# The transposed one-hots of a graph kernel: PE transposes and ACT copies, or DVE comparisons with keys from a DMA

## What is computed

```python
x_i = x[dst]                                   # (25000, 48)
x_j = x[src]
tmp = jnp.concatenate([x_i, x_j, edge_attr], axis=1)      # 48 + 48 + 32 = 128
h = jax.nn.relu(tmp @ W1 + b1)                 # (25000, 128)
msg = h @ W2 + b2                              # (25000, 48)
out = jax.ops.segment_sum(msg, dst, num_segments=100000)
y = _layernorm(x + out, axis=-1)               # eps = 1e-5
```

## Time and profile before

| | |
|---|---|
| median of 3 runs | 494.03 us |
| span of the profiled execution | 593.7 us |
| PE, PE weight loads | 430.8 us, 368.5 us busy |
| DVE, POOL, ACT | 383.0, 351.2, 292.1 us busy |
| granted TensorE clock, mean | 0.937 |
| first loads of edges, last ones | 30.2 us, 551.6 us |

### The profile page before, as it was taken

One profiled execution on the slowest core, in us unless ns is written; L12 is line 12 of the kernel. 1 busy time (PEld: TensorE's weight loads), 2 busy tenths in 40 slices (PEclk: granted clock), 3 DMA queues, 4 the chain that ended last, 5 costly groups with the idle time before them and its releaser, 6 DMA issues.

```text
span 593.7 us, 19546 instructions
## 1 busy us (share of the span) xinstructions
PE 430.8 (73%) x6796; PEld 368.5 (62%) x6796; DVE 383.0 (65%) x1105; ACT 292.1 (49%) x795; POOL 351.2 (59%) x365
## 2 busy tenths in 40 slices
PE   1013378797888878788788878787888878887891
PEld 1012367676767767676667767675776767766690
DVE  5423148676766678676667666776667756877673
ACT  2212147464555556464555545464555545554662
POOL 2056616767665666666665666666666666757522
PEclk9999999988988899898989888989889989999996
DMA  7833313444433434344444344343443434444422
GB/s 181 286 64 67 68 25 82 86 110 87 110 84 81 108 84 108 83 108 82 100 89 94 94 83 108 81 109 82 88 100 83 108 83 107 86 108 85 105 64 73
DMA packets 118243, 56.92 MB, mean 96 GB/s; under 512 B 46019, under 2 KB 117185, under 8 KB 118205
## 3 DMA queue, kind: packets, MB, share of 16 engines
q1 hardware_dynamic: 109440, 48.35, 32.2%
q0 software_dynamic: 8448, 6.50, 8.6%
q10 hardware_dynamic: 318, 1.61, 1.0%
HBM read 33.80 MB, written 22.61 MB: 95 GB/s over the span
## 4 chain that ended last, share of the span: by engine, by line
PE 66%; issue 18%; another core or an unknown queue 6%; ACT 4%; DVE 3%; DMA 1%; ACTq 0%; POOL 0%; SPq 0%; POOLq 0%; DVEq 0%
PE bank L839 14%; PE bank L827 11%; PE bank L819 10%; PE bank L779 8%; PE bank L805 8%; PE bank L858 7%; PE bank L773 7%; ACT onehot_t L899 2%; DMA next_dst_i<-in_dst_dram 1%; PE bank L851 1%; ACT sq L926 1%; ACT hid_t L915 1%; ACT cat L921 0%; ACT msg L894 0%
## 5 line engine op out<-in xcount | busy, mean ns | idle before, releaser
L732 POOL DMA_INDIRECT cat<-in_x_dram,cat x264 | 267.9, 1015 | 201.1 <-DMA cat<-edge_table 135.7
L899 ACT ACTIVATE onehot_t<-bank 128x384 bf16<-128x384 bf16 (+1 forms) x261 | 119.3, 498 | 182.1 <-remote 129.4
L1024 DVE TENSOR_REDUCE total<-bank 128x9 f32<-128x432 f32 (+1 forms) x88 | 52.8, 599 | 87.6 <-remote 86.5
L839 PE MATMUL bank<-x_low,onehot_t 128*128 128x48 bf16 (+1 forms) x782 | 86.0, 185 | 27.4 <-issue 26.9
L839 PE MATMUL bank<-x_rest,onehot_t 128*128 128x48 bf16 (+1 forms) x782 | 85.8, 186 | 26.7 <-issue 26.6
L858 PEld LDWEIGHTS bank<-w,hid_t 128*128 128x128 f32 x522 | 101.5, 208 | 4.0 <-issue 2.8
L779 PEld LDWEIGHTS bank<-ident_b,onehot 128*128 128x128 bf16 (+1 forms) x782 | 65.2, 107 | 61.4 <-issue 48.1
L839 PE MATMUL bank<-xs,onehot_t 128*128 128x48 bf16 (+1 forms) x782 | 86.6, 186 | 22.5 <-issue 22.1
L779 PE MATMUL bank<-ident_b,onehot 128*128 128x128 bf16 (+1 forms) x782 | 80.6, 236 | 24.9 <-issue 24.9
L740 POOL TENSOR_TENSOR ys<-ys,rstd 128x432 f32<-128x432 f32 (+1 forms) x88 | 80.3, 912 | 23.6 <-DVE rstd L1090 20.5
L858 PE MATMUL bank<-w,hid_t 128*128 128x48 f32 x522 | 89.9, 255 | 2.5 <-issue 2.5
(11 more groups left out here) (91 smaller groups left out, 910.8 us busy)
## 6 DMA issues: line engine op xcount, KB each, us to landing
xs<-in_x_dram SPq DMA_DIRECT2D x86, 216.0 KB
out_dram<-ys SPq DMA_DIRECT2D x86, 216.0 KB
cat<-edge_table SPq DMA_DIRECT2D x264, 17.0 KB
cat<-in_x_dram,cat POOLq DMA_INDIRECT x264
edge_table<-table_pm SPq DMA_DIRECT2D x4, 833.0 KB, 7.5
edge_pm<-in_edge_attr_dram ACTq DMA_DIRECT2D x2, 686.0 KB, 6.0
edge_pm<-in_edge_attr_dram SPq DMA_DIRECT2D x2, 686.0 KB, 6.0
edge_pm<-in_edge_attr_dram ACTq DMA_DIRECT2D x2, 91.9 KB, 7.3
```

The costliest lines, as they stand in the source:

```text
L732: pool.indirect_dma_start(cat[:, v, k, D:2 * D], None, x[:, :], bass.IndirectOffsetOnAxis(ap=cat[:, v, k, P + 1:P + 2].bitcast(I32), axis= ...
L839: last = pe.matmul(xdst_ps[:, k * D:(k + 1) * D], onehot_t[0:n, v % SMALL, k, j * P:(j + 1) * P], part[:, (k * jj + j) * D:(k * jj + j + 1 ...
L899: act.activation(onehot_t[0:n, v % SMALL, k, 0:jj * P], onehot_ps[k % 2][0:n, 0:jj * P], ACT.Copy).then_inc(onehot_t_ready, 1)
L1024: dve.tensor_reduce(total[0:n, v % SMALL, 0:blocks * jj], sums_of(g, v % SMALL), AX_X, ALU.add).then_inc(totalled, 1)
```

## The change

The transposed one-hot no longer comes from the one-hot. onehot_t[node, edge] is 1 where the edge's destination is the node, and DVE makes it by a comparison: it needs the edges' destinations along the free dimension, the same in all partitions. So the set-up part writes the destinations, each modulo 768 (two blocks, CYCLE), as float16 to a DRAM row key_line. For each block SP then loads 128 keys from key_line, spread over the 128 partitions, into keys: three more DMAs for a super, issued in turn with those of edge_table. DVE compares them with the node that a partition stands for (node_col, short_col), for two supers at once (PAIR): six comparisons of 128x384 in every second step, make_onehot_t. It stands in DVE's list where place_dst stood, second.

Since the keys are modulo two blocks, place_dst goes: edge_table holds the key in place of the destination, and make_onehot compares it with the even or the odd half of node_of. turn_onehots, turn_last_onehot, copy_onehots and copy_last_onehot leave the lists of PE and ACT, and the two PSUM banks fall free. fetch_xdst reads onehot_t in its new layout. The flag for the general path is also set if two neighbouring blocks have fewer than 128 edges together, because a key could then match a node two blocks on. The set-up part gets nine more DVE instructions ahead of the table's last column, three more ahead of the flag, one more for constants, and one DMA (key_line).

```diff
+KEY_SLOTS = 4
...
+    PAIR = 2
+    CYCLE = 2 * BLOCK
...
+    key_line = nc.dram_tensor("key_line", (ROWS,), F16, kind="Internal").ap()
...
+        keys = sb("keys", [P, KEY_SLOTS, PAIR * SUPER, P], F16)
...
-        dst_in_block = sb("dst_in_block", [P, SMALL, SUPER])
...
-        onehot_t = sb("onehot_t", [P, SMALL, SUPER, J * P], BF16)
+        onehot_t = sb("onehot_t", [P, SMALL, J, PAIR * SUPER, P], BF16)
...
             sp.wait_ge(cols_placed, 2)
+            sp.dma_start(key_line.rearrange("(p t) -> p t", p=P), key_rows_h[:, :]).then_inc(table_out, 16)
...
-            sp.wait_ge(table_out, 16 * TCH)
+            sp.wait_ge(table_out, 16 * TCH + 16)
...
+                half, pair = v % PAIR, v // PAIR
+                s, q = pair % KEY_SLOTS, pair // KEY_SLOTS + r * (BODY // PAIR // KEY_SLOTS)
                 firsts = numbers(first_edge[0:1, bass.ds(super_row(g) * 4, SUPER)])
                 for k in range(SUPER):
 
                     first = firsts[first_place(g) + min(k, blocks - 1)]
                     sp.dma_start(cat[:, v, k, 2 * D:P + META], edge_table[bass.ds(first, P), :]).then_inc(row_in[v], 16)
+                    sp.dma_start(keys[:, s, half * SUPER + k, :],
+                                 key_line[bass.ds(first, P)].rearrange("(a e) -> a e", a=1).broadcast_to([P, P])).then_inc(keys_in[s], 16)
...
+                pe.wait_ge(onehot_ready, g + 1)
...
-            def turn_block(g, v, k):
-                n, blocks, jj = shape_of(g)
-                for j in range(jj):
-                    last = pe.transpose(onehot_ps[k % 2][0:n, j * P:(j + 1) * P], onehot[:, v, k, j * n:(j + 1) * n],
-                                        ident_b[:, :])
-                last.then_inc(onehot_turned, 1)
-
-            def turn_onehots(g, r, v):
-
-                n, blocks, jj = shape_of(g)
-                pe.wait_ge(onehot_ready, g + 1)
-                if after(g, 1):
-                    pe.wait_ge(onehot_t_ready, first_block(g))
-                for k in range(min(blocks, 2)):
-                    turn_block(g, v, k)
-
-            def turn_last_onehot(g, r, v):
-
-                n, blocks, jj = shape_of(g)
-                if blocks == SUPER:
-                    pe.wait_ge(onehot_t_ready, first_block(g) + 1)
-                    turn_block(g, v, 2)
...
-                pe.wait_ge(onehot_t_ready, first_block(g) + blocks)
+                pair, half = v // PAIR, v % PAIR
+                pe.wait_ge(onehot_t_ready, g - half + PAIR)
                 for k in range(blocks):
                     for j in range(jj):
                         for i, part in enumerate(parts):
-                            last = pe.matmul(xdst_ps[:, k * D:(k + 1) * D], onehot_t[0:n, v % SMALL, k, j * P:(j + 1) * P],
+                            last = pe.matmul(xdst_ps[:, k * D:(k + 1) * D], onehot_t[0:n, pair % SMALL, j, half * SUPER + k, :],
...
-            walk(pe, ((2, turn_cat), (0, turn_onehots), (5, sums), (2, hidden), (0, turn_last_onehot), (1, fetch_xdst),
-                      (3, messages)))
+            walk(pe, ((2, turn_cat), (5, sums), (2, hidden), (1, fetch_xdst), (3, messages)))
...
-            def copy_block(g, v, k):
-                n, blocks, jj = shape_of(g)
-                act.wait_ge(onehot_turned, first_block(g) + k + 1)
-                act.activation(onehot_t[0:n, v % SMALL, k, 0:jj * P], onehot_ps[k % 2][0:n, 0:jj * P],
-                               ACT.Copy).then_inc(onehot_t_ready, 1)
...
-            walk(act, ((7, root), (2, copy_cat), (4, copy_msg), (0, copy_onehots), (6, square), (0, copy_last_onehot), (2, relu),
-                       (1, place_xdst)))
+            walk(act, ((7, root), (2, copy_cat), (4, copy_msg), (6, square), (2, relu), (1, place_xdst)))
...
-            dve.tensor_copy(table_pm[:, :, DE], dst_rows[:, 0:EC]).then_inc(cols_placed, 1)
+            note(dve.tensor_scalar(key_rows[:, :], dst_rows[:, 0:EC], N - 0.5, None, ALU.min))
+            note(dve.tensor_scalar(cycle_i[:, :], key_rows[:, :], 1.0 / CYCLE, None, ALU.mult))
+            note(dve.tensor_copy(cycle_f[:, :], cycle_i[:, :]))
+            note(dve.scalar_tensor_tensor(out=key_rows[:, :], in0=cycle_f[:, :], scalar=-float(CYCLE), in1=key_rows[:, :],
+                                          op0=ALU.mult, op1=ALU.add))
+            note(dve.tensor_scalar(cycle_f[:, :], key_rows[:, :], 0.0, float(CYCLE), ALU.is_lt, ALU.mult))
+            note(dve.tensor_tensor(key_rows[:, :], key_rows[:, :], cycle_f[:, :], ALU.add))
+            note(dve.tensor_scalar(cycle_f[:, :], key_rows[:, :], float(CYCLE), -float(CYCLE), ALU.is_ge, ALU.mult))
+            note(dve.tensor_tensor(key_rows[:, :], key_rows[:, :], cycle_f[:, :], ALU.add))
+            note(dve.tensor_copy(key_rows_h[:, :], key_rows[:, :]))
+            dve.tensor_copy(table_pm[:, :, DE], key_rows[:, :]).then_inc(cols_placed, 1)
...
+            note(dve.tensor_tensor(pair_counts[:, 0:NB - 2], first_row[:, 2:NB], first_row[:, 0:NB - 2], ALU.subtract))
+            note(dve.tensor_reduce(sparse[:, :], pair_counts[:, 0:NB - 2], AX_X, ALU.min))
+            note(dve.scalar_tensor_tensor(out=crowded[:, :], in0=sparse[:, :], scalar=P - 0.5, in1=crowded[:, :],
+                                          op0=ALU.is_lt, op1=ALU.add))
...
-            def place_dst(g, r, v):
-
+            def make_onehot(g, r, v):
                 n, blocks, jj = shape_of(g)
                 dve.wait_ge(row_in[v], 16 * SUPER * (r + 1))
-                dve.tensor_tensor(dst_in_block[:, v % SMALL, 0:blocks], cat[:, v, 0:blocks, P],
-                                  block_start[:, bass.ds(first_block(g), blocks)], ALU.subtract).then_inc(dst_counted, 1)
-
-            def make_onehot(g, r, v):
-                n, blocks, jj = shape_of(g)
-                nodes = node_of if jj == J else short_node_of
-                dve.wait_ge(dst_counted, g + 1)
                 if after(g, BODY):
                     dve.wait_ge(sum_done, g - BODY + 1)
                 for k in range(blocks):
-                    last = dve.tensor_scalar(onehot[:, v, k, 0:n * jj], nodes[:, 0:n * jj],
-                                             dst_in_block[:, v % SMALL, k:k + 1], None, ALU.is_equal)
+                    odd = (v * SUPER + k) % 2
+                    nodes = node_of[:, odd * BLOCK:(odd + 1) * BLOCK] if jj == J else short_node_of[:, :]
+                    last = dve.tensor_scalar(onehot[:, v, k, 0:n * jj], nodes, cat[:, v, k, P:P + 1], None, ALU.is_equal)
                 last.then_inc(onehot_ready, 1)
...
+            def make_onehot_t(g, r, v):
+
+                if v % PAIR:
+                    return
+                pair = v // PAIR
+                s, q = pair % KEY_SLOTS, pair // KEY_SLOTS
+                dve.wait_ge(keys_in[s], 16 * PAIR * SUPER * (r * (BODY // PAIR // KEY_SLOTS) + q + 1))
+                t = pair % SMALL
+                if after(g, PAIR * SMALL):
+                    dve.wait_ge(xdst_done, g - PAIR * (SMALL - 1))
+                blocks = sum(shape_of(g + i)[1] for i in range(PAIR)) if isinstance(g, int) and g >= NS - PAIR else PAIR * SUPER
+                full = blocks if blocks == PAIR * SUPER else blocks - 1
+                for odd in range(2):
+                    for j in range(J):
+                        last = dve.tensor_scalar(onehot_t[:, t, j, odd:full:2, :], keys[:, s, odd:full:2, :],
+                                                 node_col[:, odd * J + j:odd * J + j + 1], None, ALU.is_equal)
+                if full < blocks:
+                    for j in range(RJ):
+                        last = dve.tensor_scalar(onehot_t[0:RP, t, j, SUPER, :], keys[0:RP, s, SUPER, :],
+                                                 short_col[0:RP, j:j + 1], None, ALU.is_equal)
+                last.then_inc(onehot_t_ready, PAIR)
...
-            walk(dve, ((6, total_sum), (-1, place_dst), (-1, less_high_x), (6, centre), (-1, less_middle_x),
+            walk(dve, ((6, total_sum), (-1, make_onehot_t), (-1, less_high_x), (6, centre), (-1, less_middle_x),
```

More of the change, by code:

```diff
@@ L418, in gnn_resnorm_kernel @@
     FAR = 1 << 20
+    PAIR = 2
+    CYCLE = 2 * BLOCK
+    assert PAIR * KEY_SLOTS == BODY and (PAIR * SUPER) % 2 == 0 and BODY % PAIR == 0 and NS % PAIR == 0 and CYCLE <= 2048
     BG = 100
@@ L476, in gnn_resnorm_kernel @@
         ident_b = sb("ident_b", [P, P], BF16)
-        node_of_i = sb("node_of_i", [P, BLOCK], I32)
-        node_of = sb("node_of", [P, BLOCK], F16)
+        node_of_i = sb("node_of_i", [P, CYCLE], I32)
+        node_of = sb("node_of", [P, CYCLE], F16)
         short_node_of = sb("short_node_of", [P, REST], F16)
-        block_start = sb("block_start", [P, NB])
-        block_start_i = sb("block_start_i", [P, NB], I32)
+        node_col_i = sb("node_col_i", [P, 2 * J], I32)
+        node_col = sb("node_col", [P, 2 * J])
+        short_col_i = sb("short_col_i", [P, RJ], I32)
+        short_col = sb("short_col", [P, RJ])
+        key_rows = sb("key_rows", [P, EC])
```

(27 more changed lines are left out.)

9 lines of the change are left out of this document (4 added, 5 removed).

## The result

The changed kernel takes 628.4 us (median of 4 runs, 627.07 to 630.51) where the kernel before takes 494.25 us beside it: a ratio of 1.2742, 95% interval [1.2697, 1.2786]. The forecast was 586 us, with a range of 510 to 630. Sign and mechanism are as predicted; the size is 42 us beyond the forecast's centre, at the upper end of its range.

The account below looks back on a forecast made before the run. It took POOL (4.99 us a step) as the bound, SP 0.3 us behind; with SP's new step of 6.1 us, start 31 + 87 steps 531 - 7 without stores + tail 31 gave 586 us, range 510 to 630.

Parts of the forecast that it names:

- (c): SP gains three DMA issues a step, 1.44 us, taking its step from 4.65 to 6.09 us.
- The upper bound: SP's step at most 4.93 + 1.6 = 6.5 us, with 0.53 us between issues, giving 625 us.
- (a): PE loses nine transposes and ACT three copies a step: 0 in the steady part, 4 us gained in the tail.
- (b): DVE loses place_dst and gains three comparisons a step, 0.85 us; its step becomes 4.9 us.
- (d): DMA queues gain 3 x 128 packets a step, 28 ns each, 0.67 us an engine; counted as 0.
- (e): DVE's new wait on keys, second in its step: price 0 as long as SP doesn't fall behind.
- (f): Set-up: some ten small DVE instructions ahead of the table's DMA, counted as 1 us, bounds 0 and 4.
- The rule weighed: Skill rule on SP's DMA initiation time: by it (c) would be 0 and the time the second rival's.
- Clock: Rival: PE's clock stays at its lower level, 1.2 GHz, and PE sets the step, some 668 us; chance 0.05.
- SP cheap outside the profile: Rival: POOL stays the bound; 509 us with 0.3 us more a step from DVE's pressure, else 494; chance 0.11.
- Faster: Rival: PE in truth sets the step, so up to 48 us go: 446 to 491 us; chance 0.07.
- General path: Rival: the stricter guard sends the kernel into its general path; chance nil.

Follow-up runs that it names:

- the twins: Kernel before plus three dummy key DMAs a step on SP: 629.06 us; plus only one: 530.4 us; changed kernel with one key DMA a step: 530.9 us.
- the two with dummy loads: Kernel before plus key DMAs on SP whose data nothing uses: three a step 629.06 us, one a step 530.4 us.
- The twin: Kernel before, PE transposes and ACT copies kept, plus three dummy key DMAs a step on SP: 629.06 us.
- the best conditions: Changed kernel with store on ACT, scaling on DVE and key DMAs for the first eight groups only: 508.92 us.
- both moves: Kernel before with its store issued by ACT and its last multiplication (scaling) on DVE: 441.08 us, ratio 0.8937.

## Why the prediction was right, and where its sizes were off

- **What bounds the kernel now** (POOL 4.99 us, SP just behind, PE free): right as to SP and PE. The scaling taken from POOL gives 2.4%, SP relieved nothing, both 10.6%. What it lacked is that POOL and DVE work on each other: with the store on ACT both are full, and taking the scaling from POOL relieves both. Treating the 99.7 us of halts as the recording's was right as well: of the kernels of this case, only the one trace of before has a span unlike its ordinary time; all others agree within 1%.
- **(c) SP's price**: the mechanism was right and is shown by the twins (629.06 against 628.4; 530.4 against 530.9). The term was mis-sized in both parts. SP's step before was put at 4.65 us, joined from 3.21 and a triple of 1.44 read in the start-up; in the loop it is 4.84, because from the last load of a triple to the load of nodes there are another 0.15 us that the join left out. The three issues were put at 1.44 us (the length of a triple, which holds two distances and one short issue); in the loop they are 6.60 - 4.84 = 1.76. The upper bound, made with the distance of 0.53 (1.6 us for three), was the nearer reading of the same row. An issue inside this loop costs at least the distance between two starts, not its bar.
- **The sum**, term by term: start 30.24 us (31 predicted); from the first load of edges to the first of the last group 585.94 - 30.24 = 555.7 us (524 predicted: 87 steps of 6.39 in the mean, since the first dozen, without a store, take only 5.37 in the mean); tail 627.4 - 585.94 = 41.5 us (31 predicted). So 32 of the 41 us missed are the step, 10 the tail. The tail was the unshrunk 42.1 us of before shrunk by the factor of the whole, less 4. The variants of the kernel before, whose traces have no halts, lie between 34.1 us (scaling on DVE) and 47.0 (store on ACT), with 36.6 and 39.1 for the two with dummy loads: one factor for the whole doesn't give the tail.
- **(a)** PE's and ACT's relief at nothing in the steady part: right (PE at 0.83 of its clock and still not on the path; ACT 195.7 us busy, under 200). In the tail its 4 us don't show.
- **(b)** The new comparisons at 0.85 us for three: right (1.58 us for six, by starts). Two things were missed, both off the path here: beside POOL's scaling a triple takes 1.96 us, and with SP and POOL out of the way DVE's added work costs 0.73 us a step.
- **(d)** Transfers at 0: right. The queue has 147600 - 109440 = 38160 packets more, and their time is 0.368 x 627.4 - 0.322 x 593.7 = 39.7 us of each of 16 engines, 17 ns a packet and not the 28 ns of the bound. The same packets issued by ACT give back 60 us, so the packets don't make the 628 us.
- **(e)** The wait on the keys: DVE waits for them 57.2 us in all, as a part of waiting for SP. It has no price of its own by SP's timeline: SP sets the step and waits for others only 1.9 us in all between 90 and 588 us; 25.2 of its 25.6 us of waits for POOL stand behind the last loads. The twin can't show this, since POOL and DVE wait for its dummy loads as well (POOL 175.5 us).
- **(f)** Set-up: the first load is issued at 30.24 us, before at 30.19. The price was 0.05 us, not 1, by one trace of each.
- **The rule weighed.** The time between issues, 0.53 us in the loop, six times a step, is half of the kernel's step. The Trainium skill (DMA: Bandwidth & Descriptors, section Issuing engines are not separate DMA queues) calls that time "usually small relative to the DMA itself". Taken by its words the trace agrees: the key load issued at 302.00 us releases DVE at 305.21, 3.2 us later, six times the 0.53. What fails is the step from small to free, by which the prediction let the rule give (c) a price of 0. The 3.2 us are hidden by loading three groups ahead, the time on SP is not, and three issues of 32 KB a step are worth 135 us (493.4 to 629.06).
- **The rivals.** Clock: the granted clock fell to 0.83, and the twin with PE's full work has the same time, so PE didn't decide. SP cheap outside the profile: excluded by the twins, since each issue has its full price in ordinary executions. Its second half, DVE against POOL, is real, but here it costs DVE's time and not the kernel's: with the key loads gone a step takes 5.00 us, and the step of 5.2 that the rival had doesn't come (the 13 us between 506.85 and 494 are those of the first eight groups' key issues). Faster: excluded even under the best conditions (508.92 against 441.08). General path: not taken.

## What to carry to other kernels

An engine that only issues DMAs has a step like any other: read it by the distance of the starts of its issues inside the loop, with its register work and its reading of numbers, and compare it with the busy engines' steps before adding a single transfer. A change that takes work off two engines pays only if one of them sets the step; ask first which three engines are within 5% of it, and whether the new work lands on one of these. Where POOL and SP bound a kernel, moving one elementwise operation to DVE and one store to ACT gave 10.6%, far more than either alone (2.4% and nothing). And a variant that leaves a cost out only after a start-up still pays for it there: compare the steady steps of two runs before reading the difference of their times.

## What the hardware showed that I had not expected

- DVE is held while POOL's TENSOR_TENSOR works: in the changed kernel, between 100 and 500 us, 45 triples of L1051 that overlap one take 1.86 us in the mean and 16 that overlap none 0.77. It isn't the comparisons alone: of the 65 instructions of DVE over 1 us from 100 us on, all overlap a scaling, and 18 of them are not comparisons but TENSOR_TENSORs. POOL's scaling itself takes 0.91 us in the mean and never over 0.98. In the kernel before with three dummy loads a subtraction of 128x3 elements is the one that falls beside it, and takes 965 ns where it takes 147 with the store on ACT:

```profile
L1062 DVE TENSOR_TENSOR dst_in_block<-cat,block_start 128x3 f32<-128x3 f32 (+1 forms) x88 | 84.9, 965 | 12.7 <-DMA keys<-key_line 12.7
```

  Whether DVE delays POOL's gathers in turn stays open: beside DVE's triple and beside none they take 1.15 and 0.98 us with both moves, 1.20 and 0.95 with the store on ACT, but 0.96 and 0.99 with the scaling alone moved. The Trainium skill (SBUF — State Buffer, section Who interferes with whom) has the exclusive port pair of VectorE and GpSimd, where the one that issues first blocks the other, and not only VectorE GpSimd, as the prediction had it; the trace agrees that the two exclude each other, with VectorE as the one that pays here: 2.55 us for six where 1.58 is the price. Which of them issued first the trace doesn't tell: the held instruction of VectorE has the earlier start on record (all of those over 1 us in the changed kernel).
- One DMA issue with a computed address costs SP 0.53 us by its starts although its bar is 0.33. Behind the store's issue 2.6 us pass to the next load, 1.0 of them the reading of the three row numbers, as a piece of the chain of the step before shows:

```profile
303.93 1.00 SPq L693
```

  On ACT the reading and the triple cost 2.8 us.
- The halts of recording stood in the trace of the kernel before alone. Why only there, no run tells.
